# Third scan of a four-layer kernel: other places for the spreads of B and C, the projections and the skip products

## The reference

```
dbl = xc @ xproj_w.T
dtr, Bs, Cs = dbl[..., :dr], dbl[..., dr:dr + ds], dbl[..., dr + ds:]
dt = softplus(dtr @ dt_w.T + dt_b)
A = -exp(A_log)
def step(h, inp):                      # along the L = 1024 pixels
    dt_t, B_t, C_t, x_t = inp
    dA = exp(dt_t[..., None] * A)
    h = dA * h + (dt_t * x_t)[..., None] * B_t[:, None, :]
    y = einsum('bds,bs->bd', h, C_t)
    return h, y
y = ys + xc * Dp                       # the skip
```

## Time and profile before

| | us |
|---|---|
| three runs | 1931.17, 1936.68, 1937.81 (median 1936.68) |
| the profiled execution | 1930.74 |
| its span, first to last instruction | 1928.6 |
| first to last start of the third scan's scans | 1357.6 to 1819.4 |

### The profile page before, as it was taken

One profiled execution on the slowest core, in us unless ns is written; L12 is line 12 of the kernel. 1 busy time (PEld: TensorE's weight loads), 2 busy tenths in 40 slices (PEclk: granted clock), 3 DMA queues, 4 the chain that ended last, 5 costly groups with the idle time before them and its releaser, 6 DMA issues. The chain is left out here.

```text
span 1928.6 us, 29133 instructions
## 1 busy us (share of the span) xinstructions
PE 1523.3 (79%) x9958; PEld 777.3 (40%) x9958; DVE 1566.1 (81%) x1303; ACT 1179.5 (61%) x1807; POOL 1076.2 (56%) x700
## 2 busy tenths in 40 slices
PE   5888877999778788787888877658877877877687
PEld 2555534887333333333333333225333333333233
DVE  3788844655799999999999999543799999999754
ACT  3444465434767677676677765266677677666356
POOL 0666601000377777777777776200698898898501
PEclk8999988999899999999899998778899999999899
DMA  4000000000254444545454545200000000000001
GB/s 141 2 0 0 1 1 0 1 1 1 43 100 92 94 92 92 95 90 97 88 98 89 96 87 99 58 1 0 1 1 1 1 0 0 0 0 1 12 0 44
DMA packets 23297, 78.11 MB, mean 40 GB/s; under 512 B 3776, under 2 KB 4672, under 8 KB 22976
## 3 DMA queue, kind: packets, MB, share of 16 engines
q0 software_dynamic: 18288, 66.59, 18.3%
q1 hardware_dynamic: 4944, 10.68, 1.9%
HBM read 8.58 MB, written 2.10 MB: 6 GB/s over the span
## 5 line engine op out<-in xcount | busy, mean ns | idle before, releaser
L1274 POOL TENSOR_TENSOR s_prod<-s_ahead,s_cs 128x1024 f32<-128x1024 f32 x127 | 309.2, 2435 | 183.8 <-DVE s_back L1217 153.9
L1895 POOL TENSOR_TENSOR r_state<-r_state,r_cs 128x1024 f32<-128x1024 f32 x127 | 300.3, 2374 | 179.1 <-DVE r_state L1846 178.0
L1846 DVE TENSOR_TENSOR_SCAN r_state<-r_decay,r_pu 128x1024 f32<-128x1024 f32 x128 | 292.7, 2286 | 21.3 <-PE r_py L1692 17.4
L1214 DVE TENSOR_TENSOR_SCAN s_ahead<-s_fore,s_pu 128x1024 f32<-128x1024 f32 x128 | 292.7, 2286 | 8.6 <-ACT s_fore L1131 1.7
L1217 DVE TENSOR_TENSOR_SCAN s_back<-s_aft,s_pu 128x1024 f32<-128x1024 f32 x128 | 289.4, 2261 | 0.5 <-ACT s_aft L1141 0.5
L1765 ACT ACTIVATE r_decay<-r_pd,r_aneg 128x1024 f32<-128x1024 f32 x128 | 142.7, 1115 | 117.3 <-PE r_pd L1636 117.0
L1131 ACT ACTIVATE s_fore<-s_pd,s_aneg 128x896 f32<-128x896 f32 x128 | 129.9, 1015 | 111.0 <-PE s_pd L944 109.9
L1636 PE MATMUL r_pu<-r_partsu,selr 64*128 64x512 f32 x512 | 156.1, 425 | 41.3 <-DVE r_state L1846 38.2
L1842 DVE TENSOR_TENSOR r_pu<-r_pu,r_bs 128x1024 f32<-128x1024 f32 x128 | 155.2, 1213 | 11.8 <-PE r_pu L1636 11.6
L944 PE MATMUL s_pu<-s_partsu,selr 64*128 64x512 f32 x512 | 98.9, 464 | 77.3 <-DVE s_back L1217 73.8
L1636 PE MATMUL r_pd<-r_partsd,selr 64*128 64x512 f32 x512 | 157.6, 428 | 0.1
(11 more groups left out here) (344 smaller groups left out, 3286.2 us busy)
## 6 DMA issues: line engine op xcount, KB each, us to landing
s_ahead<-s_back POOLq DMA_DIRECT2D x127, 512.0 KB, 4.6
x_act<-in_x_dram SPq DMA_DIRECT2D x8, 256.0 KB, 5.0
out_dram<-x_act SPq DMA_DIRECT2D x16, 128.0 KB, 2.3
k_scan<-in_pack_scan_dram SPq DMA_DIRECT2D x1, 1600.0 KB, 10.0
k_fir<-in_pack_fir_dram SPq DMA_DIRECT2D x1, 1600.0 KB, 13.4
k_l<-in_pack_l_dram SPq DMA_DIRECT2D x1, 515.0 KB, 3.4
k_l<-in_pack_l_dram SPq DMA_DIRECT2D x1, 450.0 KB, 6.5
k_ln<-in_pack_ln_dram SPq DMA_DIRECT2D x3, 131.0 KB, 3.5
```

The source lines that it names most:

```text
L1214: dve.tensor_tensor_scan(ahead[:, v % 4], f, feed[:], 0.0, ALU.mult, ALU.add).then_inc(ahead_done, 1)
L1274: pool.tensor_tensor(prod[:, b], ahead[:, v % 4], cs[:, buf].rearrange("p i n -> p (i n)"), ALU.mult).then_inc(prod_done, 1)
L1846: dve.tensor_tensor_scan(state[:, v % 4], decay[:, v % 4], feed[:], 0.0, ALU.mult, ALU.add).then_inc(scanned, 1)
L1895: pool.tensor_tensor(state[:, v % 4], state[:, v % 4], cs[:, phase, q // 2], ALU.mult).then_inc(multiplied, 1)
```

## The change

The slots get a table, indexed by the old slot number: positions k=4 and k=5 keep slots 0 and 1, k=6 takes 2 and 3, k=7 takes 4, k=0 and k=1 none, k=2 takes 5 and 6, k=3 keeps 7. The projections stay at k=0 and k=1 but stand ahead of y. The two skip products, both ahead of y at k=7 until now, stand one at k=6 and one at k=0, at the end of the step. On ScalarE the Ln moves from k=2 to k=1. The names w and slot are now set per table entry.

```diff
+        SLOTS = [0], [1], [2, 3], [4], [], [], [5, 6], [7]
...
-                w = s - LAG_B
-                if live(w, UNITS):
+                begun = s - LAG_B - (u - LAG_B) % 8
+                for slot in SLOTS[(u - LAG_B) % 8] if live(begun, UNITS) else ():
                     half, phase, _, _ = cells(u - LAG_B)
-                    slot = (u - LAG_B) % 8
+                    w = begun + slot
...
-                    if k == 1 and live(s, UNITS):
-                        pe.wait_ge(relu_done, gi + 8)
-                    if k == 2 and live(s, UNITS):
+                    if slot == 5 and live(s, UNITS):
                         pe.wait_ge(lo_bc, gi + 8)
...
+                if k < 2 and live(s, UNITS) and not (isinstance(s, int) and s < EARLY):
+                    if k == 0:
+                        pe.wait_ge(s_copied, begun + 5)
+                        wait(pe, lo_bc, gi)
+                        pe.matmul(ps_m[:], wdt[:], xc[:, columns(gi, N)], start=True, stop=True).then_inc(dt_ps, 8)
+                    else:
+                        pe.wait_ge(relu_done, gi + 8)
+                        pe.matmul(ps_m[:], c["wbc"], xc[:, columns(gi, N)], start=True, stop=True).then_inc(bc_ps, 8)
...
-                    if z % 8 == 3:
-                        for chunk in range(2):
-                            pe.matmul(ps_y[:], place[:, 2 * phase + chunk],
...
+                if z % 8 in (2, 4) and live(o, UNITS):
+                    phase, chunk = cells(z)[1], z % 8 // 4
+                    pe.matmul(ps_y[:], place[:, 2 * phase + chunk], xc[:, columns(o - z % 16 + 8 * chunk, N)],
+                              start=False, stop=False, skip_group_check=True)
...
-                    act.wait_ge(one_done, gi + 8)
-                    act.activation(ln[:], one[:], ACT.Ln).then_inc(ln_done, 8)
                     act.wait_ge(ln_done, gi + 8)
                     act.activation(one[:], one[:], ACT.Copy, bias=-1.0).then_inc(grown_done, 8)
...
                     act.activation(parts_bc[:, par, 0, at], ps_m[:], ACT.Copy).then_inc(hi_bc, 8)
+                    act.wait_ge(one_done, gi + 8)
+                    act.activation(ln[:], one[:], ACT.Ln).then_inc(ln_done, 8)
```

More of the change, by code:

```diff
@@ L1678, in body @@
                         wait(pe, y_done, o - 1)
-                    if z % 8 == 3:
-                        for chunk in range(2):
-                            pe.matmul(ps_y[:], place[:, 2 * phase + chunk],
-                                      xc[:, columns(o - z % 16 + 8 * chunk, N)], start=False, stop=False,
-                                      skip_group_check=True)
                     if isinstance(o, int) and o == UNITS - 1:
```

## The result

The changed kernel takes 1923.36 us (median of 4 runs, 1919.09 to 1926.25), the kernel before beside it 1936.91; the ratio is 0.9934, interval 0.9907 to 0.9962. The profiled execution took 1924.66 us (span 1922.1), 6.1 us less than the profiled execution of the kernel before.

A forecast was written before the change was run, and what follows sets the result against it. VectorE was taken to bound the third scan, with a slightly longer closed loop after the change. Gains of 12.1 + 2.2 + 2.0 = 16.3 us gave 1914.4 from the profiled execution, 1920.4 from the median; forecast 1918, range 1907 to 1932.

The forecast's parts named there:

- PEclk under 1.00 inside the loop: Sign of being wrong: TensorE's clock below its full 2.4 GHz level within the third scan's repeating groups.
- the twelve groups: Third scan, 96 units in groups of eight: each falls from 29.07 to 28.06 us, gaining 12.1 us.
- the start: First scans of the third scan: smaller skip wait and first scan some 0.7 us earlier, gaining 2.2 us, between 0 and 4.2.
- the end: Last 23 intervals of the third scan: the 1.31 us wait is the skip pair; gain 2.0 of 2.5 us.
- The bound: Third scan: VectorE bounds it at 3.45 us per unit, 438.2 us, with 23.6 us of waits on top.
- The loop of 28.06: Closed loop through TensorE, ScalarE copy and GpSimd back to y of k=5: 28.06 us per group, above VectorE's 27.6.
- the case in which it falls: Fourth rival: TensorE's clock falls to 1.2 GHz at k=2 once per group; 30.2 us groups, 1945.7 us total; chance 0.06.
- The price of a fall: TensorE at k=2: about 3 us of steps at the lower clock take about 2.1 us more.
- The 5.9 us: Whole kernel before: the median of the runs lies 5.9 us above the profiled 1930.74, turning 1914.4 into 1920.4.
- steps 1 to 3: TensorE: projections ahead of y (k=0 3.06, k=1 3.16 us), skips off k=7 (y 1.81 earlier), two spreads at k=6 and k=2.
- step 3: TensorE: two spreads with a ScalarE copy between; k=6 takes 4.54 us, k=3 starts 5.16 behind k=2 instead of 3.64.
- The Ln: ScalarE: moving it to k=1 costs nothing; without cover at most about 0.6 us per group.

The follow-up runs named there:

- both with unread products at k=2: Matrix products nobody reads added in TensorE's waits at k=2: two in the kernel before (1930.19 us), four in the changed kernel (1911.79 us).
- GpSimd's addition: One unread 128x256 addition per group on GpSimd, against the changed kernel with four unread products at k=2: 1917.14 us; with a skip product there too: 1912.79.

## Why the prediction was right, and where it was not

The time, its range and its sign came out, and the mechanism of the loop with them. In part this is luck: the prediction's own sign of being wrong, "PEclk under 1.00 inside the loop", is there too, the groups are 27.8 or above 29 rather than 28.06, and the sum is near the truth because errors cancel. In us (the last column leaves out the time ahead of the first scan):

| | forecast | profiled pair | both with unread products at k=2 |
|---|---|---|---|
| the twelve groups | 12.1 | 4.8 | 14.4 |
| the start | 2.2 | 0.9 | 0.1 |
| the end | 2.0 | 2.4 | 1.2 |
| sum | 16.3 | 8.1 | 15.7 |

- **The bound.** VectorE with 3.45 us per unit and 23.6 us of waits on top: right. The two kernels with a skip product at k=2 are within 2.2 us of it over the twelve groups (27.78 and 27.71 against 27.6).
- **The loop of 28.06.** Its mechanism was right: GpSimd's product is released by the C copy, and GpSimd's addition lengthens the group by 0.37, or by 0.09 where the loop is shorter. Its size was 0.2 too long, 27.8 in undisturbed groups: k=6 takes 4.41 instead of 4.54, and the C copy releases GpSimd 0.11 earlier. So at full clock the term was too small, 12.1 where 14.4 were measured.
- **Start and end.** The forecast put them down to the place of the skip pair. Most of the start is the clock: held up by unread products, the kernel before wins 2.4 us there with the pair where it was. In the changed kernel the clock was low again at the start, and waits of 1.63 and 0.56 took the place of the 1.90.
- **The step that failed** is the one on the clock: "Inside the loop the longest wait that I work out is 3.01 − 1.13 − 0.50 = 1.38, at k=2, today's own", with a chance of 0.06 for the case in which it falls. The longest wait is indeed the same, and I took it for harmless because the profiled execution of before shows no fall with it. But with the skips alone moved, this one wait let the clock fall in three of twelve groups; in the changed kernel a second one of 0.69 follows it, and it fell in five. The price of a fall, put at 2.1 us, was 1.4 to 2.6; five of them make most of the 10 us between the groups of this kernel (28.67) and of the one with unread products (27.84). It was wrong to count it once in every group: it came in five of twelve. The Trainium skill ("TensorE: Matmul & The Clock Gate", Part 1: The HAM clock gate) has recent work decide the clock; the runs agree: from 1388 to 1735 us the clock is 1.00 with four unread products per group, 0.97 without. Why the clock falls in some groups and not in others with the same waits stays open.
- **Why the total held all the same.** The kernel before, it seems, loses time in the same way in most executions, which its profiled execution hid. The 5.9 us between that execution and the median, which I only carried along, were probably this in large part. That this loss and that of the changed kernel nearly cancel was luck.
- **Which part earns.** I had added the gains of steps 1 to 3 as one loop. Taken apart, the skips make most of it, 1.00 of 1.20 us per group at full clock. The other 0.20 are no more than the Ln's 0.27, so slots and projections save nothing on top, and the double spread of step 3 adds a second wait at k=2. With it came 5 falls instead of 3, and with the skips at k=7 8 falls and no gain at all; but these are counts of single executions.
- **The Ln** was costed at nothing. Its move is worth 0.27 us per group, 3.2 us in twelve groups, which the forecast left out.

## What to carry to other kernels

Where several engines hand a value round in a circle, add up the circle, and compare it with the busiest engine and with today's period; then lengthen one link to see whether the circle is the bound. When work is moved within a period, look at what the move empties as well: a wait of TensorE can cost its clock on top of its own length, and a product moved (or even an unread one added) into it pays for itself. One profiled execution can be the lucky one; compare its time with those of the timed ones before the sum is made against it.

## What the hardware showed that was not expected

- TensorE's clock fell behind waits of 1.38 and 0.69 us in five of twelve groups with the same program, and in none with waits of 0.90 and 0.22. It stayed low for 3 to 4 us in three groups and for 6 to 7 us in two. One wait of 1.38 alone also let it fall, in three of twelve groups, in the kernel with the skips alone moved.
- On GpSimd two dependent steps of 1.29 us start 1.42 apart, and an independent step of 0.62 put between two of them added only 0.40.
- Around the turn of the loop body, once in four groups, intervals between scans are 3.53 instead of 3.45 in every kernel, up to five of them in a row, without a named releaser. The cause stays open.
